# Seven block products in place of eight in the second product, shared bytes for raw and low parts, and 256-column matmuls in the first

## The reference

```python
y = einsum('bsi,boi->bso', x, weight[adapter_ids])       # stage one, per element
base_out = einsum('btd,od->bto', y, base_W) + base_b     # stage two, shared weights
logits = einsum('btd,nd->btn', y, router_W) + router_b   # 15 router columns
probs = softmax(logits); topk_p, topk_i = top_k(probs, 8)
w = einsum('btk,btke->bte', topk_p, onehot(expert_map[topk_i]))
h = einsum('btd,erd->bter', y, A)                        # 8 experts x rank 16 = 128 columns
lora = einsum('bter,eor->bto', h * w[..., None], B) * 2.0
return x + base_out + lora
```

## Time and profile before

| | |
|---|---|
| three runs | 421.62, 422.23, 425.84 us |
| span of the profiled execution | 421.1 us |
| busy: PE, DVE, ACT | 413.3, 220.0, 135.3 us |
| mean granted clock of PE | 0.996 of full speed |
| one element in the loop, stage one and stage two | 50.70 us: 22.19 and 28.51 |

### The profile page before, as it was taken

How to read it: one execution, slowest core, us unless ns; L and a number is a source line. 1 busy time by engine, 2 the same in 40 slices (tenths; PEclk the granted TensorE clock), 3 DMA queues, 4 the chain that set the end, 5 groups by cost and what they waited for, 6 DMA issues and landing times.

```text
span 421.1 us, 6443 instructions
## 1 busy us (share of the span) xinstructions
PE 413.3 (98%) x2356; PEld 390.4 (93%) x2356; DVE 220.0 (52%) x438; ACT 135.3 (32%) x236; POOL 0.8 (0%) x8
## 2 busy tenths in 40 slices
PE   6989999999999999999999999999999999999997
PEld 5879998899988999899998999989998899988996
DVE  2577858654266623676227652366424655255232
ACT  3475534630055300561015600365004540053000
POOL 0000000000000000000000000000000000000000
PEclk8999999999999999999999999999999999999999
DMA  6876966930177203771057511574016740150002
GB/s 201 287 281 215 362 238 255 339 128 0 69 252 283 95 0 121 270 256 50 0 191 269 196 42 50 194 280 173 0 50 224 280 144 0 50 199 2 0 2 100
DMA packets 20093, 64.72 MB, mean 154 GB/s; under 512 B 2418, under 2 KB 6130, under 8 KB 19186
## 3 DMA queue, kind: packets, MB, share of 16 engines
q1 hardware_dynamic: 20082, 64.57, 43.4%
HBM read 56.18 MB, written 8.39 MB: 153 GB/s over the span
## 4 chain that ended last, share of the span: by engine, by line
PE 95%; DMA 2%; DVE 1%; SPq 0%; ACT 0%; issue 0%
PE y_ps L546 26%; PE s_ps L578 16%; PE s_ps L577 16%; PE s_ps L580 16%; PE y_ps L548 13%; DMA w_raw<-in_wT 2%; PE y_ps L560 2%; PE s_ps L589 2%; PE s_ps L588 2%; PE s_ps L590 2%; PE s_ps L605 0%; DVE w_lo L385 0%; ACT s_hi L285 0%; SPq L195 0%; SPq L191 0%
## 5 line engine op out<-in xcount | busy, mean ns | idle before, releaser
L546 PE MATMUL y_ps<-x_split,w_hi 128*128 128x512 f32 x496 | 172.7, 392 | 1.2 <-DVE w_lo L385 1.2
L548 PE MATMUL y_ps<-x_split,w_lo 128*128 128x256 f32 x496 | 139.1, 280 | 0.0
L577 PE MATMUL s_ps<-s_hi,y_hi 128*128 128x392 f32 (+1 forms) x384 | 131.2, 342 | 0.0
L578 PE MATMUL s_ps<-s_lo,y_hi 128*128 128x392 f32 (+1 forms) x384 | 130.4, 340 | 0.0
L580 PE MATMUL s_ps<-s_hi,y_lo 128*128 128x392 f32 (+1 forms) x384 | 130.0, 339 | 0.0
L546 PEld LDWEIGHTS y_ps<-x_split,w_hi 128*128 128x128 f32 x496 | 92.9, 187 | 21.6 <-DVE w_lo L385 1.5
L548 PEld LDWEIGHTS y_ps<-x_split,w_lo 128*128 128x128 f32 x496 | 94.0, 190 | 0.0
L385 DVE TENSOR_TENSOR w_lo<-w_raw,w_hi 128x1024 fp32r<-128x1024 f32 x62 | 75.2, 1215 | 1.4 <-ACT w_hi L293 1.4
L577 PEld LDWEIGHTS s_ps<-s_hi,y_hi 128*128 128x128 f32 x384 | 72.2, 188 | 0.3
L578 PEld LDWEIGHTS s_ps<-s_lo,y_hi 128*128 128x128 f32 x384 | 72.2, 188 | 0.0
L580 PEld LDWEIGHTS s_ps<-s_hi,y_lo 128*128 128x128 f32 x384 | 72.1, 188 | 0.0
(11 more groups left out here) (46 smaller groups left out, 162.5 us busy)
## 6 DMA issues: line engine op xcount, KB each, us to landing
w_raw<-in_wT SPq DMA_DIRECT2D x63, 512.0 KB, 3.5
res<-in_x SPq DMA_DIRECT2D x16, 512.0 KB, 4.9
out<-res SPq DMA_DIRECT2D x15, 512.0 KB, 2.7
x_raw<-in_xT SPq DMA_DIRECT2D x7, 1024.0 KB, 5.5
c_raw<-in_base_t SPq DMA_DIRECT2D x8, 392.0 KB, 3.7
x_raw<-in_xT SPq DMA_DIRECT2D x4, 256.0 KB, 4.2
c_raw<-in_base_t SPq DMA_DIRECT2D x2, 480.0 KB, 7.4
w_raw<-in_wT SPq DMA_DIRECT2D x4, 128.0 KB, 4.4
```

What stands on the lines that cost most here:

```text
L546: nc.tensor.matmul(y_ps[:, o % 2, :], w_hi[:, slot, k, :], x_split[:, k, :, :].rearrange("p s t -> p (s t)"), start=(k == 0), stop=False)
L548: mm = nc.tensor.matmul(y_ps[:, o % 2, 0:T], w_lo[:, slot, k, :], x_split[:, k, 0, :], start=False, stop=(k == KC - 1))
L577: nc.tensor.matmul(dst, hi, s2_hi[:, k, cols], start=(k == 0), stop=False)
L578: nc.tensor.matmul(dst, hi, s2_lo[:, k, cols], start=False, stop=False)
```

## The change

1. **Stage one**: the 512-column matmul is replaced by two of 256 columns, both accumulating in the same 256 PSUM columns. `y_part` and the addition go; ACT copies PSUM to `yf` and casts it to `y_hi`.
2. **Stage two**: 464 columns (A, router, padding and 320 of base) stay plain, 8 steps of three matmuls for each tile (`plain`). The other 704 base columns are taken as two halves of 352. With the contraction halved too (4 steps each) and the two token tiles as rows, that is a 2 x 2 by 2 x 2 block product, and it is done with seven block products in place of eight (`product`, 4 steps of three matmuls of 352 columns each). It needs sums of blocks of y (`sums` after every second chunk, `fourth` after the plain products) and of base (`block_sums`, once, in element 0). A block product that serves several outputs is left in its PSUM bank: DVE adds it into `res`, then PE accumulates the next product on top, behind a wait for that addition (`x_added`, `z_added`).
3. **Memory**: the raw tile shares bytes with the low part. So SP loads a slot of the adapter only after the chunk that used it is multiplied (`y_ps_done`), and loads x of the next element only after stage one has ended.
4. **Order of element 0**: A, router, plain base columns, base blocks and B are loaded in one pass without waits on splits; see the order below.

```diff
-                    nc.tensor.matmul(y_ps[:, o % 2, :], w_hi[:, slot, k, :],
-                                     x_split[:, k, :, :].rearrange("p s t -> p (s t)"), start=(k == 0), stop=False)
-                    mm = nc.tensor.matmul(y_ps[:, o % 2, 0:T], w_lo[:, slot, k, :], x_split[:, k, 0, :],
-                                          start=False, stop=(k == KC - 1))
+                    nc.tensor.matmul(dst, w_hi[:, s, k, :], x_hi[:, k, :], start=(k == 0), stop=False)
+                    nc.tensor.matmul(dst, w_hi[:, s, k, :], x_lo[:, k, :], start=False, stop=False)
+                    mm = nc.tensor.matmul(dst, w_lo[:, s, k, :], x_hi[:, k, :], start=False, stop=(k == KC - 1))
...
+            def stage2(b, first=False):
...
+                plain(b, 1, first)
+                plain(b, 0, first)
...
+                product(x_ps, *y_block(0, 0), B00, wait_blocks=first).then_inc(x_ps_done, 1)
+                pe.wait_ge(s_lo_done, KH * b + KH)
...
+                product(z_ps, *s_block(S1), T1).then_inc(z_ps_done, 1)
+                pe.wait_ge(x_added, 4 * b + 1)
+                product(x_ps, *s_block(S2), T2, begins=False).then_inc(x_ps_done, 1)
+                pe.wait_ge(hw_done, b + 1)
...
+                product(w_ps, *y_block(1, 0), B10)
+                pe.wait_ge(x_added, 4 * b + 2)
+                product(x_ps, *s_block(S3), T3, begins=False).then_inc(x_ps_done, 1)
+                pe.wait_ge(z_added, 2 * b + 1)
+                pe.wait_ge(s4_lo_done, b + 1)
+                product(z_ps, *y_block(0, 1), B11, begins=False)
...
+                pe.wait_ge(x_added, 4 * b + 3)
+                product(x_ps, *y_block(1, 1), T4, begins=False)
+                lora_b(1, x_ps[:, 0:NH], N1).then_inc(x_ps_done, 1)
...
+            def block_sums(j):
+                raw = [st_raw[:, j, i, :] for i in range(7)]
+                dve.wait_ge(st_in[j], 32)
+                nc.vector.tensor_tensor(raw[T3], raw[B11], raw[T1], ALU.subtract)
+                nc.vector.tensor_tensor(raw[T1], raw[T1], raw[B00], ALU.subtract).then_inc(t1_done, 1)
+                dve.wait_ge(t1_done, j + 1)
+                nc.vector.tensor_tensor(raw[T2], raw[B11], raw[T1], ALU.subtract).then_inc(t2_done, 1)
+                dve.wait_ge(t2_done, j + 1)
+                nc.vector.tensor_tensor(raw[T4], raw[B10], raw[T2], ALU.subtract).then_inc(st_done, 1)
+            def blocks_lo(j):
+                dve.wait_ge(st_hi_done, j + 1)
+                nc.vector.tensor_tensor(st_lo[:, j, :, :], st_raw[:, j, :, :], st_hi[:, j, :, :], ALU.subtract).then_inc(st_lo_done, 1)
...
+            def blocks_hi(j):
+                act.wait_ge(st_done, j + 1)
+                nc.scalar.copy(st_hi[:, j, :, :], st_raw[:, j, :, :]).then_inc(st_hi_done, 1)
...
+            def element(b, last=False):
...
+                add_bias(b)
+                fourth(b)
+                if not last:
+                    make_x_lo(b)
+                fourth_lo(b)
+                stage2(b, lambda: None)
...
+            sp.wait_ge(y_ps_done, 1)
+            load_w(id0, 4)
+            load_plain(0)
+            sp.wait_ge(y_ps_done, 2)
+            load_w(id0, 5)
+            load_plain(1)
+            load_blocks(0)
+            sp.wait_ge(y_ps_done, 3)
+            load_w(id0, 6)
+            load_blocks(1)
+            sp.wait_ge(y_ps_done, 4)
+            load_w(id0, 7)
+            load_blocks(2)
+            load_blocks(3)
```

More of the change, by code:

```diff
@@ L32 @@
 F32_CHUNKS = 2
-C_SLOTS = 4
 LORA_SCALE = 32.0 / 16.0
@@ L48, in adaln_ffn_kernel @@
     AR = ER + NR + 1
[L50 to L59, removed]
+    KH = KC // 2
+    NP = 320
+    NH = (D - NP) // 2
+    PL = AR + NP
+    PLAIN, N1, N2 = slice(0, NP), slice(NP, NP + NH), slice(NP + NH, D)
+    assert PL <= 512 and OC == 2 * KH and NT == 2
+    ORDER = [o for j in range(KH) for o in (j, j + KH)]
     PIECES = 4
@@ L158, in adaln_ffn_kernel, with w_uses, split @@
         block = ctx.enter_context(nc.Block())
[L161 to L183, removed]
+        def w_uses(b, c):
+            return (OC // W_SLOTS) * b + c // W_SLOTS + (0 if c % W_SLOTS == 0 else 1)
+        def split(b, c):
+            return OC * b + c - F32_CHUNKS + 1
         @block.sync
@@ L264, in _ @@
[L264 to L271 removed]
+            sp.dma_start(b_raw[:, :], b_t).then_inc(b_in, 16)
+            for t in range(NT):
+                load_res(0, t, first=True)
+            id1 = adapter(1)
@@ L273, in _ @@
+            for c in range(W_SLOTS):
+                sp.wait_ge(y_ps_done, W_SLOTS + c + 1)
+                load_w(id1, c)
+            sp.wait_ge(x0_lo_done, PIECES)
+            load_x(1, first=True)
+            store_element(0)
             with sp.Fori(1, NB - 1) as b:
@@ L466, in make_y_sum, with add @@
[L466 to L486 removed]
+            def add(t, cols, ps):
+                return nc.vector.tensor_tensor(res[:, t, cols], ps, res[:, t, cols], ALU.add)
@@ new lines, in product @@
+            def product(ps, hi, lo, block_of, begins=True, wait_blocks=False):
+                dst = ps[:, 0:NH]
+                for j in range(KH):
+                    if wait_blocks:
+                        pe.wait_ge(st_lo_done, j + 1)
+                    nc.tensor.matmul(dst, hi(j), st_hi[:, j, block_of, :], start=begins and j == 0, stop=False, skip_group_check=not begins)
+                    nc.tensor.matmul(dst, hi(j), st_lo[:, j, block_of, :], start=False, stop=False, skip_group_check=not begins)
+                    mm = nc.tensor.matmul(dst, lo(j), st_hi[:, j, block_of, :], start=False, stop=(j == KH - 1),
+                                          skip_group_check=not begins)
+                return mm
@@ new lines, in y_block, with s_block, lora_b @@
+            def y_block(half, t):
+                return [(lambda j, y=y: y[:, half * KH + j, t * P:(t + 1) * P]) for y in (y_hi, y_lo)]
+            def s_block(i):
+                return [(lambda j, s=s: s[:, j, i, :]) for s in (s_hi, s_lo)]
+            def lora_b(t, dst, cols, begins=False):
+                skip = not begins
+                nc.tensor.matmul(dst, hwt_hi[:, t, :], b_hi[:, cols], start=begins, stop=False, skip_group_check=skip)
+                nc.tensor.matmul(dst, hwt_hi[:, t, :], b_lo[:, cols], start=False, stop=False, skip_group_check=skip)
+                return nc.tensor.matmul(dst, hwt_lo[:, t, :], b_hi[:, cols], start=False, stop=True, skip_group_check=skip)
```

639 lines of the change are left out of this document (344 added, 295 removed).

## The result

| | before | changed |
|---|---|---|
| median of the runs | 421.93 us (4 runs) | 451.56 us (450.51 to 452.68, 4 runs) |
| span of the profiled execution | 421.1 us | 450.5 us |
| one element in the loop | 50.70 us: 22.19 + 28.51 | 49.73 us: 23.03 + 26.70 |
| start of element 1 | 63.02 us | 96.60 us |

The account below looks back on a forecast made before the run. PE was taken to bound the kernel. Span 421.1, plus 36.1 us in element 0, minus 7 x 1.64 in the loop, plus 2.4 of waits, gave 448.1; the median forecast was 448 us, range 437 to 457.

Parts of the forecast that it names:

- What bounds the kernel: Whole kernel: PE is busy 98% of the span and never waits in the loop, so its instructions set the cost.
- Prices of stage two: Loop, stage two: 464 columns cost 0.209 us and 352 cost 0.159, 26.6 us in all, -1.9 us per element.
- Price of 256 columns: Loop, stage one: 192 matmuls of 256 columns at 0.117 us take 22.5 us against 22.2, +0.3 us per element.
- The rival in which the weight load bounds narrow matmuls: Stage one: a third weight load per step does not hide, +75 us, about 523 us; chance 1%.
- The loop's wait: Loop, stage two: PE waits 0.4 us for DVE's first addition, in six elements 2.4 us.
- (a) Loads: Element 0, stage one: adapter chunks 6 and 7 land late, at 27.5 and 31; it ends at 37.0, not 34.4.
- (b) Blocks: Element 0, after stage one: serial block rounds of about 7.1 us each; the last block is ready at 71.2.
- (c) Behind the last round: Element 0, after the last block: DVE work, PE products and last low parts sum to 24.9 us before element 1.
- Half clock: After element 0's two long PE gaps: 3 us at half speed each, 1.5 lost, 3.0 us in all (bounds 0 and 5).
- The sum: Whole kernel: 421.1 + 36.1 - 7 x 1.64 + 2.4 = 448.1 us of span.
- The third rival: Loop: x comes late in every element, PE waits some 2.6 us more six times, 464 us; chance 5%.
- The first rival: Element 0: block preparation is hidden, all eight elements gain 1.64 us, 409 us; even if element 0 loses 11.5; chance 4%.

Follow-up runs that it names:

- The last version: The version that stopped, with element 1's chunk-4 load issued ahead of element 0's stores and SP's element 1 program written out: 428.25 us, 1.0119 of the kernel before.
- the version that stopped: Changed kernel with early next low parts, overlapping block rounds, adapter chunks first, early masks, `fourth` behind gates, late bias: 430.63 us, 1.0174 of the kernel before.

## Why the prediction was right, step by step

- **What bounds the kernel.** Right: PE has no spare time in the loop, and element 0 decides.
- **Prices of stage two.** 464 columns 0.211 for 0.209, 352 columns 0.160 for 0.159, stage two 26.70 for 26.6. Right.
- **Price of 256 columns.** This term was mis-sized: 0.117 predicted, 0.120 measured, in the kernel before as well. The line through 240 and 392 columns rested on one spacing of 240 read as 0.11; at two digits it carried an error of 5%, and 192 matmuls in each element make 0.6 us of 0.003. Stage one costs 23.03, not 22.5: 3.8 us over seven elements. The rival in which the weight load bounds narrow matmuls (523 us) is out. The Trainium skill's 81 and 131 ns ("TensorE: Matmul & The Clock Gate", "Back-to-back issue gap") don't agree with the 0.120, 0.160 and 0.211 of this trace.
- **The loop's wait.** Predicted 0.4 us for the first addition, six times. In element 4, whose stage two began at 271.62, DVE and PE were

```profile
285.03 0.52 DVE L507 TENSOR_TENSOR res<-x_ps,res 128x352 f32<-128x352 f32 x1
```

```profile
285.60 0.43 PE L662 MATMUL x_ps<-st_hi,s_hi 128*128 128x352 f32 x1
285.86 0.32 PE L663 MATMUL x_ps<-st_lo,s_hi 128*128 128x352 f32 x1
```

  The addition came at +13.4, not +14.3, and PE at +14.0 as predicted. It lost 0.1 us there (0.03 ahead of the first and 0.10 between two starts that are 0.16 apart elsewhere), where I had said 0.4. The step was the right one to watch: with 512 columns in stage one the same wait is 2.65 us. The sum of the loop was -9.1 us by my terms and is -7.0.
- **(a) Loads.** ACT's casts of chunks 6 and 7, in the form of the earlier trace rows:

```profile
28.16 1.04 ACT L332 CAST w_hi<-w_raw 128x1024 fp32r<-128x1024 f32 x1 [4.18 <-DMA w_raw<-in_wT]
...
31.19 1.04 ACT L332 CAST w_hi<-w_raw 128x1024 fp32r<-128x1024 f32 x1 [0.86 <-DMA w_raw<-in_wT]
```

  28.2 and 31.2 for 27.5 and 31; stage one ended at 37.9, not 37.0.
- **(b) Blocks.** A pitch of 7.03 for 7.1, the last block at 71.1 for 71.2. Right, and with the rounds overlapping it came 9.4 us earlier. The lower bound was wrong, though: with no late load I had the last block at 62.2, and the version with the adapter's chunks first, whose stage one ended at 34.15, had it at 68.0.
- **(c) Behind the last round.** 25.5 us for 24.9. DVE reached the first addition after 6.5 us and PE went on after 7.1, not 7.8; PE needed 14.4 from there, not 12.6, with the clock at 0.50 in 79 to 82; then 4.0 for the low parts of element 1, not 4.5. Half clock was charged at 3.0 us for both gaps; it cost about 1.8 in element 0 (where it stayed away, PE needed 12.8) and 2.8 in element 1, and the experiments show that neither is fixed: the one went from nothing to 2.8, the other from 1.4 to 2.8 behind the same gap of 4.02. In effect element 1 begins at 99.4, predicted 99.1.
- **The sum.** Span 450.5 for 448.1: 0.3 more in element 0, 2.1 less gained in the loop. Errors there went against each other, 3.8 us for the price of 256 columns and 0.7 for stage two against 2.4 for the wait. The 0.3 of element 0 is luck in part as well: the clock cost 1.6 more than I charged, and against it stood 0.7 less for DVE ahead of the first addition, 0.5 less for the last low parts and 0.1 for the blocks. With the 1 us taken off for overlap on DVE, the forecast stood 3.6 us under the measured median.
- **The third rival's price.** By its own rule (each us of x behind T + 8.8 is one of PE), x at T + 11 costs 2.2 us in six elements, 461 and not 464. It did not come to pass: the first addition was early, not late, and PE waits for no x in the loop.
- **The first rival's turning point.** The kernel was to break even if element 0 lost no more than the loop gives. The last version loses 13.8 us there and gains 8.2: it still is 1.3% slower by its spans. How early the last block would have to be ready wasn't measured.

## What to carry to other kernels

A change that saves PE 2% in each of a few elements must be costed first where its tables are made: read the stretch before the loop from its own timeline, with the order of each engine, and ask of every new operation what stands behind it. In a stretch where two engines hand work to and fro, write the producer of round j + 1 ahead of the consumer of round j; one swap gave 10 us here, about 9 of it by the earlier blocks and 1 by the clock in element 1. A new dependence of PE on DVE makes all that stands ahead of it on DVE part of the path, an addition that used to be free included.

## What was not expected of the hardware

- A stop of PE cost more than its length, by an amount that varied: 4.02 us idle ahead of element 1 was followed by 5 us and more at a granted clock of 0.50 and cost 2.8 us besides, and the same 4.02 us cost 1.4 and 1.6 besides in two other versions; 1.75 us idle was followed by 0.64 and 0.79 and cost 1.7 besides. Behind the 2.3 to 2.4 us idle at the first addition the clock fell to 0.50 in three versions and stayed at 1.00 in one.
- A subtraction of 352 float32 elements took 0.93 to 3.43 us on GpSimd, 0.52 on DVE, and DVE's large subtractions took 3.67 us in the mean for 2.72 while GpSimd worked.
- SP issued element 1's first load at 83.25 in the version that stopped, 2.5 us after it had issued the stores (79.51 to 80.7), with nothing left to wait for but what the loop looks up. Which part of that was the loop's entry wasn't measured.
